# A decoder layer on one core: values through a DRAM scratch, x transposed and q formed a step ahead, gate scans and other VectorE work reordered

## What is computed

```python
# 1 attention: 16 heads of 32, softmax over the heads of one token (not over tokens)
q, k, v = x @ Wq.T + bq, x @ Wk.T + bk, x @ Wv.T + bv
qk  = einsum('bshd,bstd->bsht', q, k) / sqrt(32)
out = einsum('bsht,bstd->bshd', softmax(qk), v)      # then a reshape and @ Wo.T + bo
# 2 mLSTM against ctx: gates ig, fg from [q, k, v]; cumulative sum of log_sigmoid(fg),
#   a running maximum over tokens, D = exp(log_D - max), C = (q k^T / sqrt(32)) * D,
#   h = (C / normaliser) v, normalised per head
# 3 a choice among 8 small experts per token, low-rank update, bias
```

## Time and profile before

| | |
|---|---|
| median of three runs | 1725.87 us |
| profiled execution, its own time | 1729.01 us |
| its span | 1727.5 us |
| mean granted TensorE clock | 0.976 |
| busy share: TensorE, VectorE, ScalarE, GpSimd | 90%, 80%, 49%, 54% |
| DMA queue, share of 16 engines | 24.1% |

### The profile page before, as it was taken

How to read it: one execution, slowest core, us unless ns; L and a number is a source line. 1 busy time by engine, 2 the same in 40 slices (tenths; PEclk the granted TensorE clock), 3 DMA queues, 4 the chain that set the end, 5 groups by cost and what they waited for, 6 DMA issues and landing times.

```text
span 1727.5 us, 67777 instructions
## 1 busy us (share of the span) xinstructions
PE 1550.4 (90%) x27491; PEld 1222.5 (71%) x27619; DVE 1378.1 (80%) x3401; ACT 854.6 (49%) x2385; POOL 931.3 (54%) x1232
## 2 busy tenths in 40 slices
PE   0788899899999999999999999999999999999964
PEld 0566777677777777777777777777777777777752
DVE  4355788788888888888888888888888888888875
ACT  2044544545554555455545545554555455545552
POOL 1024555546655665566556555655565556556653
PEclk9899999999999999999999999999999999999985
DMA  4021222222222222222222222222222322222210
GB/s 153 25 76 63 77 93 76 77 95 73 83 87 98 73 82 88 96 75 81 90 88 82 80 91 79 91 75 96 74 94 76 98 73 87 84 98 73 79 57 31
DMA packets 53829, 141.14 MB, mean 82 GB/s; under 512 B 8767, under 2 KB 10431, under 8 KB 45578
## 3 DMA queue, kind: packets, MB, share of 16 engines
q1 hardware_dynamic: 53770, 140.31, 24.1%
HBM read 122.98 MB, written 17.30 MB: 81 GB/s over the span
## 4 chain that ended last, share of the span: by engine, by line
PE 80%; issue 7%; ACT 6%; DVE 4%; POOL 1%; SPq 1%; DMA 0%; POOLq 0%; ACTq 0%; DVEq 0%
PE bank L358 16%; PE bank L359 13%; PE bank L361 13%; PE bank L350 6%; PE quad L422 5%; PE quad L409 4%; PE quad L468 4%; PE bank L480 4%; PE bank L503 4%; PE bank L448 4%; PE quad L490 3%; DVE VT L862 2%; ACT Hs L649 2%; ACT VG L586 2%; ACT cT L602 1%
## 5 line engine op out<-in xcount | busy, mean ns | idle before, releaser
L746 POOL TENSOR_TENSOR ex<-ex,w_rec 128x512 f32<-128x512 f32 x64 | 67.0, 1047 | 595.0 <-DVE w_rec L902 595.0
L642 ACT ACTIVATE Dx<-Mb,a_col 128x128 f32<-128x128 f32 x1024 | 311.6, 390 | 3.4 <-DMA Mb<-m_rows 3.4
L766 POOL TENSOR_TENSOR h_rs<-h_ve,half_neg 128x16 f32<-128x16 f32 x64 | 187.7, 2933 | 40.0 <-DVE h_ve L979 40.0
L612 ACT ACTIVATE x1T<-bank 128x512 f32<-128x512 f32 x64 | 38.2, 597 | 308.9 <-PE bank L350 308.9
L961 DVE SCALAR_TENSOR_TENSOR Dx<-quad,Dx 128x512 f32<-128x512 f32 x256 | 158.9, 682 | 12.2 <-PE quad L468 4.6
L751 POOL TENSOR_SCALAR_AFFINE_SELECT Dx<-Dx 128x512 f32<-128x512 f32 x256 | 160.2, 639 | 3.5 <-ACT Dx L642 3.5
L780 POOL TENSOR_TENSOR rs<-ve,half_neg 128x1 f32<-128x1 f32 x192 | 104.9, 546 | 69.4 <-DVE ve L923 67.2
L358 PE MATMUL bank<-wq_high,x_high 128*128 128x512 f32 x256 | 117.3, 458 | 3.6
L358 PE MATMUL bank<-wv_high,x_high 128*128 128x512 f32 x256 | 113.1, 442 | 1.6 <-issue 1.6
L358 PE MATMUL bank<-wk_high,x_high 128*128 128x512 f32 x256 | 113.0, 441 | 0.0
L422 PE MATMUL quad<-PT,VG 32*32 32x32 f32 x8192 | 83.7, 202 | 29.1 <-ACT VG L586 18.4
(11 more groups left out here) (166 smaller groups left out, 4375.9 us busy)
## 6 DMA issues: line engine op xcount, KB each, us to landing
Mb<-m_rows SPq DMA_DIRECT2D x64, 1024.0 KB, 4.7
xb<-in_x SPq DMA_DIRECT2D x256, 64.0 KB
xr<-in_x SPq DMA_DIRECT2D x64, 256.0 KB, 3.9
cb<-in_ctx SPq DMA_DIRECT2D x64, 256.0 KB, 2.6
out_dram<-yo SPq DMA_DIRECT2D x64, 256.0 KB, 3.9
Dx<-in_wq SPq DMA_DIRECT2D x4, 256.0 KB, 4.5
Dx<-in_wk SPq DMA_DIRECT2D x4, 256.0 KB, 5.4
Mb<-in_wv SPq DMA_DIRECT2D x4, 256.0 KB, 6.0
```

Of the source, the lines that this page charges most:

```text
L642: last = go(Dx[t.parity()][:, j, n, :], Mb[t.parity()][:, h, :], ACT.Exp, bias=a_col[t.parity()][:, h:h + 1], scale=-1.0)
L766: tt(h_rs[:], h_ve[:], half_neg[:], ALU.pow).then_inc(s.hrs_sb, 1)
```

## The change

V: `p_v` now works on the newest tile a, in bank 7, and ScalarE copies it to `v_sb`. SyncE stores it to a DRAM scratch (`store_v`) and reads it back (`load_VG`) in the layout that `a_O` wants, in runs of 32 floats. VectorE's `p_VT`, TensorE's `p_VG` and ScalarE's `p_VG` are gone. `p_xT` goes to the head of the step on TensorE and ScalarE, `p_low` to the head on VectorE, and `p_q` takes the place of `p_v` between `m_HT` and `m_H`; `p_v` takes that of `p_q`. K's columns are laid out in another order, with the masks of `pairs` to match.

ScalarE's step is cut at another point (`m_gs`, `m_softplus`, `x_LT`, `m_HT`, `a_exp` are now written at the head of the next step), and `p_v` comes after `x_x2T`.

VectorE: `m_gsum` and `m_scan` now come at the head of the step, after `p_low` and still ahead of `a_max`; `r_stats` moves from between them to behind `a_rec`, then come `p_QT`, `a_PT`, `x_choose`, `r_norm`; `x_gate` comes ahead of `r_y`.

GpSimd: `m_c1` comes ahead of `r_pow`. `WARM` is 62 where it was 27.

```diff
-WARM = 27
+WARM = 62
 ...
+            def store_v(t):
+                sp.wait_ge(s.v_sb, upto(t))
+                sp.dma_start(v_dram[t.parity()], v_sb[:]).then_inc(s.v_out, 16)
+            def load_VG(t):
+                sp.wait_ge(s.v_out, stored(t.older(-1)))
+                sp.wait_ge(s.O_ps, upto(t, 1))
+                source = v_dram[t.parity()].rearrange("(u m) (h d) -> (m h) u d", m=8, d=D)
+                sp.dma_start(VG[:].rearrange("p w c d -> p (w c) d"), source).then_inc(s.v_in[t.parity()], 16)
 # SyncE step: load_x, store_v(a), load_res, store, load_VG(a), spread_M, load_ctx
...
             def p_v(t):
-                pe.wait_ge(s.fn1_sb, upto(t, 4))
-                bias(4, 2)
-                product(4, x_high, x_low, 2, False).then_inc(s.v_ps, 1)
+                pe.wait_ge(s.acol_sb, upto(t, 2))
+                bias(7, 2)
+                product(7, x_high, x_low, 2, False).then_inc(s.v_ps, 1)
...
             def a_O(t):
-                pe.wait_ge(s.VG_sb, upto(t))
+                pe.wait_ge(s.v_in[t.parity()], landed(t, 1))
...
             def m_gate(t):
+                pe.wait_ge(s.v_sb, upto(t, -1))
...
             def x_Y(t):
+                pe.wait_ge(s.Hs_sb, upto(t, -3))
...
 # TensorE step, after: p_xT(a) m_gate(c) a_S(b) m_HT(d) p_q(a) m_H(d) m_cT(b) m_aT(c)
 #   x_Y(g) a_O(b) p_v(a) x_x2T(e) a_proj(b) p_k(a) m_QK(c) m_x1T(b) x_F(e) x_LT(f)
...
 # GpSimd step
                 if c.real():
                     r_nn(c)
+                if b.real():
+                    m_c1(b)
+                if c.real():
                     r_pow(c)
...
                 if b.real():
-                    m_c1(b)
                     m_mask(b, 2)
...
 # VectorE step, after: p_low(a) m_gsum(c) m_scan(c) a_max(b) a_sub(b) a_sum(b) a_rec(b)
 #   r_stats(e) p_QT(a) a_PT(b) x_choose(f) r_norm(d) x_y3(g) r_var(d) r_x2(e) a_low(b)
 #   x_stats(g) x_gate(f) r_y(d) a_r1(b) a_stats(b) a_x1(b) p_KT(a) m_C(c) x4 x_shift(e)
```

More of the change, by code:

```diff
@@ L237, in bass_decoder @@
         four = "Dx_sb Dm_sb C_sb".split()
-        two = "x_in c_in r_in mb_in".split()
-        semaphores = {n: sem(n) for n in once + each + ["y_out", "m_out"]}
+        two = "x_in c_in r_in mb_in v_in".split()
+        semaphores = {n: sem(n) for n in once + each + ["y_out", "m_out", "v_out"]}
         semaphores |= {n: [sem(f"{n}{j}") for j in range(4)] for n in four}
@@ L277, in steps @@
                 dma = {(n, k): eng.snap(u * (16 * n) + 16 * n * k) for n in (1, 4) for k in range(-1, 2)}
-                dma |= {("out", k): eng.snap(u * 32 + 16 * k) for k in range(-LAGS, 2)}
+                dma |= {("out", k): eng.snap(u * 32 + 16 * k) for k in range(-LAGS, 3)}
                 for k in range(2):
@@ L329, in step @@
                     load_x(n2)
+                if a.real():
+                    store_v(a)
                 if n1.real():
@@ L334, in step @@
                     store(f)
+                if a.real():
+                    load_VG(a)
                 if c.real():
@@ L415, in a_O @@
                 pe.wait_ge(s.PT_sb, upto(t))
-                pe.wait_ge(s.VG_sb, upto(t))
-                edge(pe, t, (s.Hs_sb, 3), (s.sub_sb, 0), *[(s.C_sb[j], 2) for j in range(4)])
+                pe.wait_ge(s.v_in[t.parity()], landed(t, 1))
+                edge(pe, t, (s.Hs_sb, 2), (s.sub_sb, 0), *[(s.C_sb[j], 2) for j in range(4)])
                 for v in range(4):
@@ L532, in step @@
                 b, c, d, e, f, g = [a.older(n) for n in range(1, 7)]
+                if a.real():
+                    p_xT(a)
                 if c.real():
@@ L538, in step @@
                     m_HT(d)
-                if b.real():
-                    p_v(b)
+                if a.real():
+                    p_q(a)
                 if d.real():
@@ L581, in p_xT, with p_v @@
                 go(chunks(x_high), bank[5][:], ACT.Copy).then_inc(s.xhigh_sb, 1)
[L583 to L586, removed]
+            def p_v(t):
+                act.wait_ge(s.v_ps, upto(t))
+                if t.regs is not None or t.k >= 1:
+                    act.wait_ge(s.v_out, stored(t))
+                go(v_sb[:], bank[7][:], ACT.Copy).then_inc(s.v_sb, 1)
             def a_exp(t):
@@ L694, in step @@
                 b, c, d, e, f, g = [a.older(n) for n in range(1, 7)]
+                if a.real():
+                    p_xT(a)
+                if c.real():
+                    m_gs(c)
+                    m_softplus(c)
+                if g.real():
+                    x_LT(g)
+                if d.real():
+                    m_HT(d)
+                if b.real():
+                    a_exp(b)
                 if d.real():
@@ L717, in step @@
                     x_x2T(e)
+                if a.real():
+                    p_v(a)
                 if c.real():
@@ L859, in _, with turn @@
             red = nc.vector.tensor_reduce
-            def turn(dst, b):
-                return nc.vector.transpose(dst[:].rearrange("p (g h n) -> p h g n", h=H, n=2), bank[b][:])
+            def turn(dst, b, order):
+                return nc.vector.transpose(dst[:].rearrange(order + " -> p h g n", h=H, n=2), bank[b][:])
             def p_QT(t):
@@ L866, in p_QT @@
                 edge(dve, t, (s.S_ps, 1))
-                turn(QT, 4).then_inc(s.QT_sb, 1)
+                turn(QT, 4, "p (g h n)").then_inc(s.QT_sb, 1)
             def p_KT(t):
@@ L871, in p_KT @@
                 edge(dve, t, (s.S_ps, 1))
[L872 to L877, removed]
+                turn(KT, 6, "p (g n h)").then_inc(s.KT_sb, 1)
             def p_low(t):
@@ L1126, in step @@
                 b, c, d, e, f, g = [a.older(n) for n in range(1, 7)]
+                if a.real():
+                    p_low(a)
+                if c.real():
+                    m_gsum(c)
+                if c.real():
+                    m_scan(c)
                 if b.real():
@@ L1134, in step @@
                     a_rec(b)
+                if e.real():
+                    r_stats(e)
+                if a.real():
+                    p_QT(a)
+                if b.real():
+                    a_PT(b)
+                if f.real():
+                    x_choose(f)
                 if d.real():
                     r_norm(d)
-                if b.real():
-                    p_VT(b)
-                    a_PT(b)
+                if g.real():
+                    x_y3(g)
                 if d.real():
                     r_var(d)
[L1142 to L1145, removed]
                 if e.real():
                     r_x2(e)
+                if b.real():
+                    a_low(b)
                 if g.real():
                     x_stats(g)
-                if b.real():
-                    a_low(b)
+                if f.real():
+                    x_gate(f)
                 if d.real():
                     r_y(d)
[L1154 to L1157, removed]
                 if b.real():
```

54 lines of the change are left out of this document (14 added, 40 removed).

## The result

The changed kernel takes 1791.57 us (median of four runs, 1790.24 to 1793.02) against 1725.4 us for the kernel before on the same chip: a ratio of 1.038, interval 1.0362 to 1.0398. It is slower by 66 us, and the forecast of 1786 us was 5.6 us short.

What follows compares the result with a forecast made beforehand. A one-step ring through TensorE, VectorE and GpSimd bounds the kernel: 0.61 - 0.26 - 0.12 + 1.35 - 0.57 = +1.01 us per step, +57 us over some 57 tiles, +60 with WARM: 1786 us against the median 1725.87, range 1732 to 1840.

Steps and rivals of the forecast that it cites:

- The ring: a_x1, VectorE to the reciprocals, GpSimd's score to rs1, a_x1: sets the step, +1.01 us to 25.8 us.
- A: Rival: the ring does not close and TensorE decides, 24.4 us per step, 1706 us in all; chance 0.13.
- B: Rival: x_gate stays long, its lines blocked in the new place too; step 27.3 us, 1871 us; chance 0.04.
- C: Rival: GpSimd's pow excludes VectorE, so x2 and r_y wait; step 28.4 us, 1934 us; chance 0.02.
- rival D: No change: the values' DMA, the lost turn and the longer ring cancel, 1726 us; chance 0.04.
- TensorE's waits: TensorE waits ahead of m_QK and m_x1T about 2 us per step, p_v 0.35 and a_O 0.5 us.
- First half of the ring: a_x1 to GpSimd's score: 12.44 us before, changed by +0.61, -0.26 (gs wait), -0.12 (wait ahead of m_C) and +1.35.
- x_choose late, +1.35: VectorE's x_choose behind the reciprocal delays GpSimd's score: reciprocal to score 3.21 us, not 1.86, +1.35 us.
- p_low, +0.61: p_low on VectorE between x_shift and m_gsum, inside the ring: +0.61 us, filling the 0.26 us wait for gs.
- Second half: GpSimd's score to a_x1, 12.37 us before: -0.57 from pow's wait, 0 to +0.15 from h_ve beside m_c1.
- x_gate short: VectorE's x_gate ahead of r_y, beside pow, takes 1.2 to 1.4 us instead of 3.04; r_y2 hardly waits.
- WARM, +3: 35 more warm-up matmuls ahead of the first step: +3 us taken, bounds -1 to +4.

Runs made afterwards that it cites:

- Experiment 2: Changed kernel with x_choose moved back ahead of a_sum, under the exponential: 1731.8 us, ratio 1.0034.
- experiment 1: Changed kernel with p_low behind m_gsum instead of ahead of it: 1772.57 us, ratio 1.0268.
- experiment 3: Changed kernel with m_c1 back behind r_y2 on GpSimd: 1812.26 us, ratio 1.0492.
- experiment 5: Changed kernel with K turned into the old order of columns (computes wrong scores): 1772.43 us, ratio 1.0279.
- experiment 4: Changed kernel with the values' load from the scratch issued twice, first into an unread buffer: 1790.83 us, ratio 1.0367.
- experiment 6: Kernel before with x_choose alone moved behind a_PT: 1874.48 us; with ScalarE's x_exp also moved behind its a_O: 1869.52 us.
- experiment 9: m_c1 behind mask 3, on changed kernel with p_low behind m_gsum and x_choose early: 1719.16 us; also WARM 27: 2122.58 us; kernel before with m_c1 moved: 1744.03 us.
- experiment 8: Changed kernel with p_low behind m_gsum, x_choose ahead of a_sum, and GpSimd's rs1 rsqrt ahead of masks 0 and 1: 1737.97 us, ratio 1.0078.

## Why the prediction was right, point by point

- **The ring** is shown. Experiment 2 takes one link out and gets 60 us back; experiments 1, 3 and 5 change other links and move the time by their own price; experiment 4 doubles something off the ring and moves nothing. Rivals A, B, C and D are out.
- **TensorE's clock** had no term, and in the changed kernel it needed none. In 15 of 50 steps the granted clock is 0.93 in the mean and a_r1 waits 2.0 to 2.4 us for a_proj, not 0.8, but these steps are as long as the others, 25.95 to 25.98 us. rs1 stands behind the masks in GpSimd's queue and covers the delay. In experiments 2 and 6 the same fall of the clock reached the step.
- **TensorE's waits** were less well placed. The forecast has about 2 us ahead of m_QK and m_x1T. In the step of the rows above it is 0.77 and 0.17 us; 0.74 lies ahead of a_O (0.5 forecast) and 0.43 ahead of p_v (0.35 forecast). The sum does not rest on it.
- **First half of the ring**: forecast 12.44 + 0.61 - 0.26 - 0.12 + 1.35, some 14.0 us; measured 14.10. Two errors nearly cancel in it. From a_x1 to the reciprocal it is 829.35 - 818.32 = 11.03 us, where the terms give 10.81: K's turn, taken over at its old 0.70, is 1.07 us, and a_x1 to m_C is 1.68 us where 1.46 was forecast. K's turn is the one VectorE instruction of the diff with a new layout, and I priced only its place. In return the stretch from the reciprocal to the score is 3.07, not 3.21.
- **x_choose late, +1.35**: measured +1.21 between reciprocal and score, 1.16 in the step. The largest term by far.
- **p_low, +0.61**: right net of the wait that it fills (0.41 in the mean by experiment 1, forecast 0.35).
- **Second half**: forecast 11.8 to 11.95, measured 11.88. h_ve was held up by m_c1 for 0.74 us (bound 0 to 1.0), but pow stands behind m_c1 and started 0.11 us after its end. The surprise is pow itself, 3.24 us where it took 2.93. The rows tie it to x2's norm (line 1006). In the changed kernel 63 of 64 pows have that norm starting 0.1 us ahead of them and take 3.2 us; the one without it, the first, takes 2.93. In the kernel before, the norm starts 0.6 to 1.3 us into pow in all steps but the first, and all 64 pows take 2.93 or 2.94. I moved neither by itself, so this is a reading of the rows.
- **x_gate short**: 837.09 to 838.65, 1.56 us instead of 3.04 (forecast 1.2 to 1.4); its first key, line 1031 before, has a median of 0.227 us. x2's norm took 0.53 us although pow started 0.09 us after it. By the Trainium skill, SBUF — State Buffer, section SBUF: two separate sides, a VectorE instruction in a two-port mode or with two SBUF inputs and a GpSimd instruction hold each other off for a whole instruction. Here that is seen beside GpSimd's plain long instructions (h_ve, line 1041). Beside the power of 128 by 16 it is not: x2's norm ran in 0.54 us in its middle before, and the key with its SBUF inputs in 0.23 us here.
- **The values' scratch costs nothing**: shown by experiment 4, as long as its place in SyncE's queue keeps its lead. Experiment 9 shows what happens when it does not.
- **WARM, +3**: VectorE's first x_low moved from 55.53 to 58.87 us, +3.3. Less of it lasted: the first a_x1 is 2.0 us later than before and the eleventh 1.4 us, though other parts of the change act in these steps too.
- **The number of steps** was too high and the step too short. From the eleventh a_x1 to the last there are 53 steps, and each costs 1.16 us more: 61.7 us, where the forecast had 57 times 1.01. With the 1.4 us ahead of them and 0.7 us behind the last a_x1 that is the 63.8 us between the two spans, 1727.5 and 1791.3. The medians differ by 66.2 us, because the profiled execution of before was 3.6 us above its median and that of the changed kernel 1.5. So the closeness of 1786 to 1791.57 owes something to two sizes that erred in opposite ways; the mechanism and the largest terms do not.
- **The range**, 1732 to 1840, leaves out rival D (1726) too, so 0.23 of the chances and not 0.19.

Experiments 6, 8 and 9 went less well than the forecast. Each was priced by one ring. In 8 and 9 a second wait was within a microsecond of it, and in 6 TensorE's clock doubled the loss.

## What to carry to other kernels

Where engines wait for each other through in-order queues, look for the ring of one step and add up its links: an instruction's cost is decided by what its result starts, not by its engine's busy share. Four small instructions in the wrong place cost 60 us here, and a 256 KB round trip through DRAM in a good place cost nothing. Before moving work into an idle stretch, ask what its completion releases, on the DMA queue too, and how near the second ring is. When a step is longer than the links add up to, compare single steps of one trace, with their granted clocks: in experiment 6 that separated the two payments.

## What was not expected of the hardware

- VectorE's 32 by 32 turn of 128 by 512 took 1.07 us into the new layout of K and 0.70 us into the old one.
- GpSimd's power of 128 by 16 took 2.93 us in the kernel before and 3.24 us in the changed one, where x2's norm on VectorE starts 0.1 us ahead of it.
- TensorE's granted clock was 0.55 over the 3.8 us behind a wait of 1.48 us, and 1.00 behind one of 1.55 us in the next step; the step was 27.79 us with the first and 26.31 us with the second.
- The same loop ran at a granted clock of 1.00 or of 0.87 from 400 to 1600 us, 1719 or 2123 us in all, after 62 or 27 warm-up matmuls.
